# First dense stage of a four-layer graph network: both additions of x and h on VectorE, x in six buffers, another order of loads, stores and products

## What is computed

```python
h   = jnp.maximum(_layernorm(x, axis=-1), 0.0)
# _L0_gnn_ref(h, ...):
xj  = h[col] * norm[:, None]            # norm = dis[row] * dis[col]
agg = jax.ops.segment_sum(xj, row, num_segments=n)
out = jax.nn.relu(agg @ W.T + b)
x   = x + (h + out)
```

## Time and profile before

| | us |
|---|---|
| three runs | 7486.71, 7510.91, 7485.44 |
| median | 7486.71 |
| span of the profiled execution, first to last instruction | 7497.3 |
| first dense stage in it, first load to the next stage's first instruction | 1678.0 to 2239.7 |

### The profile page before, as it was taken

How to read it: one execution, slowest core, us unless ns; L and a number is a source line. 1 busy time by engine, 2 the same in 40 slices (tenths; PEclk the granted TensorE clock), 3 DMA queues, 4 the chain that set the end, 5 groups by cost and what they waited for, 6 DMA issues and landing times. The chain is left out here.

```text
span 7497.3 us, 113351 instructions
## 1 busy us (share of the span) xinstructions
PE 3517.3 (47%) x18429; PEld 2636.7 (35%) x18429; DVE 5174.6 (69%) x20258; ACT 2902.8 (39%) x7124; POOL 5022.1 (67%) x4720
## 2 busy tenths in 40 slices
PE   7655256646658888850005777200786233333000
PEld 1111155546656666640004555100564122222000
DVE  7999488877778888877776777322674355555554
ACT  0366111117764333335555666100232255554222
POOL 0377578874447777776657774577787677776577
PEclk9756599998889999985557888655998555555555
DMA  7488577769983333346669999322897333333343
GB/s 288 161 289 288 150 137 142 141 124 277 286 251 92 92 91 92 90 109 175 176 169 349 361 363 330 97 52 50 301 343 241 94 102 103 103 103 95 120 136 114
DMA packets 1168522, 1326.52 MB, mean 177 GB/s; under 512 B 231275, under 2 KB 968789, under 8 KB 1157938
## 3 DMA queue, kind: packets, MB, share of 16 engines
q1 hardware_dynamic: 961680, 1002.76, 41.8%
q0 software_dynamic: 206768, 323.00, 17.8%
HBM read 706.30 MB, written 646.54 MB: 180 GB/s over the span
## 5 line engine op out<-in xcount | busy, mean ns | idle before, releaser
L690 POOL DMA_INDIRECT dense<-t_xs,ends x784 | 789.0, 1006 | 360.3 <-issue 182.2
L1810 PE MATMUL ps<-dense,w 128*128 128x256 f32 x3136 | 731.1, 386 | 187.2 <-DVE dense L1519 160.2
L530 POOL DMA_INDIRECT t_src<-tot,sidx x392 | 626.8, 1599 | 183.4 <-issue 94.6
L1810 PEld LDWEIGHTS ps<-dense,w 128*128 128x128 f32 x3136 | 581.4, 190 | 305.2 <-DVE dense L1519 193.8
L1732 PE MATMUL ps<-oneh_c,oneh_p 128*128 128x395 f16 x1568 | 458.7, 430 | 276.2 <-DVE oneh_c L867 267.1
L762 ACT ACTIVATE estd<-emv,epsc 128x2 f32<-128x2 f32 (+1 forms) x588 | 174.1, 296 | 1044.2 <-DVE emv L745 1044.2
L1519 DVE SCALAR_TENSOR_TENSOR dense<-xT 128x256 f32<-128x256 f32 x1568 | 544.6, 419 | 3.6 <-ACT xT L1991 3.4
L665 POOL DMA_INDIRECT t_yacc<-dense,gq x392 | 456.1, 1164 | 129.6 <-issue 111.1
L690 POOL DMA_INDIRECT dense<-t_y,ends x392 | 372.9, 951 | 251.2 <-DVE ends L1612 164.7
L628 POOL DMA_INDIRECT out_rows<-dense,sidx x392 | 387.9, 990 | 183.1 <-issue 111.6
L628 POOL DMA_INDIRECT t_xs<-dense,sidx x392 | 398.5, 1017 | 123.7 <-issue 65.2
(11 more groups left out here) (327 smaller groups left out, 12111.5 us busy)
## 6 DMA issues: line engine op xcount, KB each, us to landing
dense<-t_xs SPq DMA_DIRECT2D x78, 1320.0 KB
dense<-in_x SPq DMA_DIRECT2D x156, 640.0 KB
t_xs<-dense SPq DMA_DIRECT2D x98, 528.0 KB, 4.5
t_xs<-hb SPq DMA_DIRECT2D x78, 660.0 KB, 6.1
t_src<-dense SPq DMA_DIRECT2D x99, 512.0 KB, 6.3
t_sum<-dense SPq DMA_DIRECT2D x98, 512.0 KB
t_src<-dense SPq DMA_DIRECT2D x78, 640.0 KB, 3.3
dense<-t_src SPq DMA_DIRECT2D x78, 640.0 KB
```

Of the source, the lines that this page charges most:

```text
L530: gp.indirect_dma_start(t_src, bass.IndirectOffsetOnAxis(ap=sidx[:, p.k, c:c + 1], axis=0), tot[:, p.k, c, :], None, compute_op=ALU.add).t ...
L690: gp.indirect_dma_start(rows[:, p.k, c, :], None, table, bass.IndirectOffsetOnAxis(ap=gidx[:, p.k, c:c + 1], axis=0)) \
L1810: i = nc.tensor.matmul(ps[:, o:o + 2 * P], w1[:, k, :], xm[:, p.w, k, :], start=(k == 0), stop=(k == R - 1))
```

## The change

`node_loop` is replaced in this stage by `wide_loop`, whose loop body is six blocks long (`WIDE = 6`) and whose part written out before the loop is 18 blocks on SP and PE and 12 on the engines without a lag. `x` has six places: the three that it had and three more areas of the same buffer, which nothing else uses in this stage. POOL's addition is gone. DVE makes `oa = max(oa, 0) + h` in place and signals `gain`, then `hb = oa + x` and signals `res`. SP's order in iteration `b` is: store of block `b - 4`, sums of `b`, x of `b`; x waits for `res` of six blocks before. DVE's wait for the store of three blocks before stands ahead of its last addition, no longer ahead of the products. PE's order is: products of `b - 1`, then transposes of `b`. DVE's function has lag 0. On ACT `h` is a function of its own behind the copy of the turned sums, and waits for `gain` of three blocks before where it waited for `res`.

```diff
+class Wide:
+
+    def __init__(self, r, u):
+        while u < 0:
+            r, u = r - 1, u + WIDE
+        self.r, self.u = r, u
+        self.b = r * WIDE + u
+        self.k, self.n = u % SLOTS, r * 2 + u // SLOTS
+
+def wide_loop(eng, *stages):
+
+    most = max(lag for _, lag in stages)
+    peeled = (2 * WIDE + most + WIDE - 1) // WIDE
...
+    for b in range(peeled * WIDE):
+        at(b)
+    with eng.Fori(peeled, NB // WIDE) as r:
+        for u in range(WIDE):
+            for fn, lag in stages:
+                fn(Wide(r, u - lag), P)
...
         xin = [area(i) for i in range(3)]
+        xin0 = xin + [area(9 + i) for i in range(3)]
...
-                if needed(b - SLOTS + 1):
-                    sp.wait_ge(L0["xh"].sem, L0["xh"].after(b - SLOTS + 1))
-                sp.dma_start(xin[u][0:p], rows_of(x, b, p)).then_inc(L0["ld"][u].sem, 16)
...
-            node_loop(sp, (conv0_load, 0), (conv0_store, 3))
+            def conv0_x(w, p):
+                if needed(w.b - WIDE + 1):
+                    sp.wait_ge(L0["res"].sem, L0["res"].after(w.b - WIDE + 1))
+                sp.dma_start(xin0[w.u][0:p], rows_of(x, w.b, p)).then_inc(X0["load"][w.u].sem, 16)
+
+            def conv0_sums(w, p):
+                if needed(w.b - SLOTS + 1):
+                    sp.wait_ge(L0["tr"].sem, L0["tr"].after(w.b - SLOTS + 1))
+                sp.dma_start(ain[w.k][0:p], rows_of(t_src, w.b, p)).then_inc(L0["lda"][w.k].sem, 16)
...
+            wide_loop(sp, (conv0_store, 4), (conv0_sums, 0), (conv0_x, 0))
...
-            def conv0_xh(r, u, p):
-                b = r * SLOTS + u
-                gp.wait_ge(L0["h"].sem, L0["h"].after(b + 1))
-                gp.tensor_tensor(ob_h[u][0:p], xin[u][0:p], ob_h[u][0:p], ALU.add).then_inc(L0["xh"].sem, 1)
-            node_loop(gp, (conv0_xh, 0))
...
-                v.wait_ge(L0["xh"].sem, L0["xh"].after(b + 1))
-                nc.vector.scalar_tensor_tensor(out=hb[u][0:p, :, 0:D], in0=oa[u][0:p], scalar=0.0, in1=ob_h[u][0:p],
-                                               op0=ALU.max, op1=ALU.add).then_inc(L0["res"].sem, 1)
+                v.wait_ge(L0["h"].sem, L0["h"].after(b + 1))
+                nc.vector.scalar_tensor_tensor(out=oa[u][0:p], in0=oa[u][0:p], scalar=0.0, in1=ob_h[u][0:p],
+                                               op0=ALU.max, op1=ALU.add).then_inc(L0["gain"].sem, 1)
+                if needed(w.n):
+                    v.wait_ge(L0["sto"][u].sem, L0["sto"][u].after(w.n * 16))
+                v.wait_ge(X0["load"][w.u].sem, X0["load"][w.u].after(w.r * 16 + 16))
+                v.wait_ge(L0["gain"].sem, L0["gain"].after(b + 1))
+                nc.vector.tensor_tensor(hb[u][0:p, :, 0:D], oa[u][0:p], xin0[w.u][0:p], ALU.add).then_inc(L0["res"].sem, 1)
...
-            node_loop(v, (conv0_rest, 1))
+            wide_loop(v, (conv0_rest, 0))
...
-            node_loop(pe, (conv0_turn, 0), (conv0_mm, 1))
+            wide_loop(pe, (conv0_mm, 1), (conv0_turn, 0))
...
-            node_loop(a, (conv0_first, 0))
+            wide_loop(a, (conv0_first, 0), (conv0_h, 0))
```

More of the change, by code:

```diff
@@ L131, in node_loop_back, with at @@
                 fn(r - back if back else r, u - lag + back * SLOTS, P)
+    for b in range(NB, NB + 1 + most):
+        at(b)
+WIDE = 2 * SLOTS
+assert NB % WIDE == 0
+class Wide:
[8 more added lines that the diff above has]
+    peeled = (2 * WIDE + most + WIDE - 1) // WIDE
+    def at(b):
+        for fn, lag in stages:
+            if 0 <= b - lag <= NB:
+                fn(Wide((b - lag) // WIDE, (b - lag) % WIDE), PT if b - lag == NB else P)
+    for b in range(peeled * WIDE):
+        at(b)
+    with eng.Fori(peeled, NB // WIDE) as r:
+        for u in range(WIDE):
+            for fn, lag in stages:
+                fn(Wide(r, u - lag), P)
     for b in range(NB, NB + 1 + most):
@@ L463, in gnn @@
         R0 = phase("runs", NPAIR, "", SC)
-        L0 = phase("node", NB + 1, "nm h tr trc mm z xh res",
-                   {"ld": slots(16), "lda": slots(16), "sto": slots(16)})
+        L0 = phase("node", NB + 1, "nm h tr trc mm z gain res", {"lda": slots(16), "sto": slots(16)})
+        X0 = phase("rows", NB + 1, "", {"load": [16 * len(range(u, NB + 1, WIDE)) for u in range(WIDE)]})
         E1 = phase("edge", NPAIR, "ring bn mv std rs nb h tx txc masked xw relu back", GP)
@@ L967, in _, with conv0_store @@
             end_phase(sp, SP)
-            def conv0_load(r, u, p):
-                b = r * SLOTS + u
-                if needed(b - SLOTS + 1):
-                    sp.wait_ge(L0["xh"].sem, L0["xh"].after(b - SLOTS + 1))
-                sp.dma_start(xin[u][0:p], rows_of(x, b, p)).then_inc(L0["ld"][u].sem, 16)
[L974 to L983, removed]
-            node_loop(sp, (conv0_load, 0), (conv0_store, 3))
+            def conv0_x(w, p):
[6 more added lines that the diff above has]
+                sp.dma_start(ain[w.k][0:p], rows_of(t_src, w.b, p)).then_inc(L0["lda"][w.k].sem, 16)
+            def conv0_store(w, p):
+                sp.wait_ge(L0["nm"].sem, L0["nm"].after(w.b + 1))
+                sp.wait_ge(L0["res"].sem, L0["res"].after(w.b + 1))
+                sp.dma_start(t_xs[bass.ds(w.b * BR, p * K), XW1:2 * XW1].rearrange("(p k) f -> p k f", k=K), hb[w.k][0:p]) \
+                    .then_inc(L0["sto"][w.k].sem, 16)
+            wide_loop(sp, (conv0_store, 4), (conv0_sums, 0), (conv0_x, 0))
             stored(sp, L0, 16)
@@ L1467, in _, with conv0_rest @@
             end_phase(v, VE)
[L1469 to L1472, removed]
+            def conv0_rest(w, p):
+                b, u = w.b, w.k
                 v.wait_ge(L0["mm"].sem, L0["mm"].after(b + 1))
@@ L1765, in _, with conv0_turn, conv0_mm @@
             end_phase(pe, PE)
[L1767 to L1771, removed]
+            def conv0_turn(w, p):
+                pe.wait_ge(L0["lda"][w.k].sem, L0["lda"][w.k].after(w.n * 16 + 16))
+                if needed(w.b):
+                    pe.wait_ge(L0["trc"].sem, L0["trc"].after(w.b))
                 for k in range(K):
-                    i = nc.tensor.transpose(ps[:, k * P:k * P + p], ain[u][0:p, k, :], ident[0:p, 0:p])
+                    i = nc.tensor.transpose(ps[:, k * P:k * P + p], ain[w.k][0:p, k, :], ident[0:p, 0:p])
                 i.then_inc(L0["tr"].sem, 1)
[L1776 to L1780, removed]
+            def conv0_mm(w, p):
+                pe.wait_ge(L0["trc"].sem, L0["trc"].after(w.b + 1))
+                if needed(w.b):
+                    pe.wait_ge(L0["z"].sem, L0["z"].after(w.b))
                 for k in range(K):
-                    i = nc.tensor.matmul(ps[0:p, ZC + k * P:ZC + (k + 1) * P], fT[u][:, k, 0:p], w0t[:, :],
+                    i = nc.tensor.matmul(ps[0:p, ZC + k * P:ZC + (k + 1) * P], fT[w.k][:, k, 0:p], w0t[:, :],
                                          start=True, stop=True)
@@ L1959, in turned, with conv0_first, conv0_h @@
                                      func, bias=bias).then_inc(signal.sem, 1)
[L1961 to L1964, removed]
+            def conv0_first(w, p):
+                turned(L0["trc"], w.b, p, fT[w.k], K, L0["tr"], L0["mm"])
+            def conv0_h(w, p):
+                b, u = w.b, w.k
+                a.wait_ge(X0["load"][w.u].sem, X0["load"][w.u].after(w.r * 16 + 16))
                 if needed(b - SLOTS + 1):
-                    a.wait_ge(L0["res"].sem, L0["res"].after(b - SLOTS + 1))
+                    a.wait_ge(L0["gain"].sem, L0["gain"].after(b - SLOTS + 1))
                 for k in range(K):
-                    i = nc.scalar.activation(ob_h[u][0:p, k, :], xin[u][0:p, k, :], ACT.Relu,
+                    i = nc.scalar.activation(ob_h[u][0:p, k, :], xin0[w.u][0:p, k, :], ACT.Relu,
                                              bias=mean_r[0:p, bass.ds(b * K + k, 1)],
@@ L1971, in conv0_first @@
                 i.then_inc(L0["h"].sem, 1)
-                if needed(r):
-                    a.wait_ge(L0["sto"][u].sem, L0["sto"][u].after(r * 16))
+                if needed(w.n):
+                    a.wait_ge(L0["sto"][u].sem, L0["sto"][u].after(w.n * 16))
                 nc.scalar.activation(hb[u][0:p, :, D], dis[1][0:p, bass.ds(b * K, K)], ACT.Copy).then_inc(L0["nm"].sem, 1)
```

## The result

Four runs of the changed kernel took 7439.4 to 7463.4 us, median 7446.2, against 7498.8 for the kernel before beside them; the ratio is 0.9924, 95% interval 0.9907 to 0.9941. A second series gave 0.9943 (0.9924 to 0.9962). The forecast was a gain of 0.3%; it is 0.6 to 0.8%, about twice that or more, and above the 0.5% that I had called measurable.

What follows compares the result with a forecast made beforehand. A ring of latencies close above a nearly full DMA was taken to bound the first dense stage. Steady blocks gaining 20.5 us plus 2.5 us at the start, 23 us, took the 7486.7 us median to 7464, range 7444 to 7496.

Steps and rivals of the forecast that it cites:

- The ring: First dense stage: `res` of j to `res` of j+3 via sums load and PE's list, 21.0 us, 7.0 a block.
- The floor of the transfers: Steady blocks of the first dense stage: DMA never starved moves 306 GB/s, so a block takes at least 6.49 us.
- the third rival: First dense stage: 306 GB/s is only demand; block falls to compute's 6.1 us or so, 7422 us; chance 7%.
- the mixture of clocks of before: PE in the first dense stage: 32% of time at 1.2 GHz, 68% at 2.4; compute needs 6.4 us a block.
- my 6.65: Forecast steady block in us, first dense stage, between 6.49 and 6.92: 0.27 us less over 76 blocks, 20.5 us.
- the transfers are no bound: Rival, first dense stage: 306 GB/s is only demand; block falls to 6.1 us or so, 7422 us; chance 7%.
- Its 5.8 us a block: DVE in the first dense stage: ten instructions and two passes of 1.49 us take 5.8 us, against 5.7 before.
- It costs nothing as long as a block takes 6.5 us: Addition moved to DVE: its 5.8 us a block stays under the transfers, so the added pass is free.
- The clock: PE's granted clock in the first dense stage: 0.84 before, 0.8 to 0.9 expected if the forecast is right.
- The rival that it makes the kernel slower: PE's transposes, copy, products take 8.3 us at 1.2 GHz; more time there gives 7512 to 7592 us; chance 7%.
- x in six places: x buffers of the first dense stage: gain only at the start, 2.5 us of a 5 us DMA pause, bounds 0 and 5.

Runs made afterwards that it cites:

- e1: Kernel before with only PE's order changed (products of b-1, then transposes of b): stage 495.0 us against 561.4, ratio 0.9936.
- e2: Kernel before with only SP's order changed (sums loaded ahead of x): stage 525.1 us against 561.4, ratio 0.9955.
- e7: Kernel before with both PE's and SP's orders changed, all else as before: stage 471.9 us against 561.4, ratio 0.9875.
- e4: Changed kernel with nine tenths of the computing left out from block 6 on, all transfers kept: stage 448.1 us, 355 GB/s, one run.
- e6: Changed kernel plus twelve unused transposes on PE behind each block's transposes: stage 473.1 us against 509.5, ratio to the kernel before 0.9885.
- e5: Changed kernel with x + h back on POOL and one pass on DVE: stage 476.0 us against 509.5, ratio to the kernel before 0.9882.
- e9: Kernel before with both orders changed, plus twelve unused PE transposes behind each block's transposes: stage 460.5 us, ratio 0.9874.
- e10: Changed kernel with x in three places instead of six: stage 506.7 us against 509.5, one run.

## Why the prediction was wrong

**The ring: right.** That one round over three blocks, from `res` of j to `res` of j+3 through the load of the sums and PE's list, set the old 6.9 us, is shown three times: e1, e2 and e7 change nothing but orders and take 66, 36 and 90 us. With PE's order changed the holes of the DMA went, and PE's wait for `t_src` fell to 36.2 us (e1) and, with both orders, to nothing (e7).

**The floor of the transfers: the step that failed.** "I take that as the floor of the transfers", 306 GB/s and 6.49 us, was read off one stretch without a hole, because its share was printed as 1.02; a shorter one of the same trace, 1991 to 2007 us, already ran at 313 GB/s. It was no floor: that stretch was fed by the same ring and showed what the ring asked for. The same column prints 1.06 at 319 GB/s, 1.09 at 327 and still 1.09 at 355 (e4). The 5.6 us that e4 measured stood in the third rival's paragraph, and I put it aside because the earlier trace rows did not reach it. With 5.60 us in the sum compute would have been the only bound: 6.4 us by the mixture of clocks of before, 0.5 less over 76 blocks, some 40 us. The rest is the mixture: with the measured 22% of the time at 1.2 GHz the same formula gives 6.2, and 6.25 was measured. The 0.16 us between the floor and my 6.65, put there for two bounds close together, fell with the floor. Steady blocks gained 51.0 us where I had 20.5. The rival "the transfers are no bound" was what happened, 6.25 us against its 6.1, and it had 7%; the row that spoke for it, loads at over 410 GB/s, was given too little weight, since half of my argument against it was the share.

**DVE.** Its 5.8 us a block was right to 0.05 us (5.84 in the timeline, 5.79 in e6), as were 1.49 us for both passes. "It costs nothing as long as a block takes 6.5 us" was right as put, and wrong with the block at 6.25: e5 prices it at 33 us. I did not ask what the change would give without it.

**The clock.** 0.89 instead of 0.84, inside what I expected. That it sits on top of DVE's time, 36 us of the stage, follows from e6; part of these 36 us and of the 33 of the DVE pass are the same, as e9 shows. The rival that it makes the kernel slower did not come.

**x in six places.** No use in the steady state, as put, e10. At the start I had 2.5 us, it was 0.8. The DMA's slices of 1681 to 1721 us show the loads running 14 slices instead of 11, and the pause behind them still four slices long, as in the earlier trace rows:

```profile
GB/s 0 133 348 394 420 364 423 420 415 425 420 420 420 425 215 10 0 0 0 0 199 295 222 369 277 297 374 326 182 202 288 415 402 326 289 197 304 403 411 346
```

The next loads, of block 4, stand behind the store of block 0 in SP's list, so they wait for its `res`, 18.6 us into the stage; before, those of block 3 left at POOL's first addition. What the longer list of loads gave, the order took back.

## What to carry to other kernels

Before work is moved between engines to relieve a ring, look whether the ring closes over an order in a queue that could be another: here two swapped pairs of lines gave 90 us and the addition moved to DVE took 33 back. A DMA rate read from a stretch in which something else sets the pace is a demand, not a ceiling, whatever the share says; the ceiling needs the transfers with the computing taken out. And a bound just below the one that is removed must be priced at the new period, not at the old.

## What was unexpected in the hardware

The printed share of the DMA engines does not tell how near the limit is: 1.02 at 306 GB/s, 1.09 at 327 and 1.09 at 355. Near the highest rates SP's own issue of the sums grows: between 1710 and 2100 us it took 3.70 us on the mean in e4 (355 GB/s) and 3.29 in e9 (349). It does not follow the rate alone, since it took 1.11 us before (286 GB/s) and 0.39 in e1 (327); what else decides it is open. The additions of DVE and POOL that held each other up to 4.16 and 4.24 us before did not meet at all in e1 and once in e7. And 1.5 us of useless transposes a block on PE shortened the stage by 36 us.
